# Layer 1 of a two-layer token network by seven half-size products in place of eight, with x1 kept in DRAM

## The chip, the cores and the metric

One core of a Trainium2 chip runs the kernel. The metric is the device time of one execution in microseconds (us). The engines are PE (TensorE), DVE (VectorE), ACT (ScalarE), POOL (GpSimd) and SP (SyncE, which here only issues DMAs).

## The reference

2048 tokens (8 rows of 256) of 1024 features pass two residual layers. Everything is fp32.

```python
# layer 0, per row of 256 tokens, with a language id per row
base = x @ W.T                                  # W 1024 x 1024
logits = x @ Wr.T + 5.0 * one_hot(language_id)  # 8 experts
gates = top-2 of logits, softmax over the two, scattered to 8
h = x @ A.T                                     # A: 8 experts x 16 x 1024
lora = (h * gates) @ B.T
x1 = x + base + 2.0 * lora
# layer 1: one 1024 x 1024 matrix of 16 per row, by adapter id
out = x1 + x1 @ weight[adapter_id].T
```

## The kernel before, in words

**Precision.** PE multiplies in a reduced fp32 (fp32r). Every operand is split into a high part (ACT, a copy that rounds, L487) and a low part (DVE, the difference, L356), and a product is three: high x high, high x low, low x high (`products`, L562 to L566).

**Order of the work.** The tokens go in 4 chunks of 512 (`NCH`). Per chunk PE does the features (L568: h and logits, 4 tiles of 128 tokens x 8 slices, one product with the high part of the tokens against both halves of the factors, 272 columns, and one with the low part, 136 columns), then 8 output tiles of W0 (`base_tile`, L583, 8 x 3 products of 512 columns each) with a low-rank part (`lora_tile`, L600, 3 products each), then layer 2 for two rows: 8 outputs of 8 x 3 products with 512 columns (L621 to L635). x1 comes transposed out of layer 1's PSUM, is split from there by ACT (L507) and DVE (L443), and stays on chip for layer 2. The residuals need no addition: POOL adds the identity to every block of W0 and W1 (`add_ones`, L291).

**Operands.** SP loads a block of 128 rows of a matrix or of the tokens as four DMAs of 128 KB (L244 to L256), into one of four raw slots (`RAW`). DVE turns it in 32 x 32 squares (L349), then the block is split. W0 is loaded and turned again for each chunk; its tiles and those of W1 share a ring of three groups of four blocks. `FIRST`, `AFTER_GATES`, `AFTER_L0` and `after_l1` (L68 to L79) give one order of blocks, which SP, POOL, DVE and ACT all follow; each engine runs its list in order and waits on semaphores.

**Gates.** Once per chunk ACT and DVE turn the feature sums of 4 token tiles into gated h (`make_gates`, L398 to L436); PE transposes it (L611), ACT and DVE split it (L529, L449).

**Start.** 37 identity products in plain fp32 (L561), whose result nobody reads, run until the first operands are there.

## Time and profile before

| | us |
|---|---|
| median of 3 runs | 424.11 (423.76 to 424.12) |
| profiled execution, span from first to last instruction | 423.0 |
| PE busy | 414.4 |
| DVE busy | 314.1 |
| ACT busy | 163.1 |
| POOL busy | 59.5 |

DMA moved 68.52 MB, mean 162 GB/s. No time of the profiled execution other than its span is given. Products overlap: a product's row shows its latency, and the next one starts before it ends, so the rhythm is read from the starts. A busy share near 100% says that an engine always had something in flight, not that it could do no more. A line such as L356 is that of the helper, and stands for all blocks.

### The profile page before, as it was taken

What the parts mean: (1) busy time and instruction counts of PE and PEld (TensorE: products, weight loads), DVE (VectorE), ACT (ScalarE), POOL (GpSimd) and SP (SyncE); (2) the same over time, 40 slices, a digit from 0 to 9 for tenths busy, and PEclk for the clock granted to TensorE, in tenths of its full rate; (3) what the DMA queues carried; (4) which work ended last, traced back from release to release, by engine and by line L of the source; (5) the groups of instructions that cost most, each with busy time, mean ns of one, the idle gap of its engine ahead of it and who ended that gap; (6) DMA issues with size and microseconds to landing.
All of it is one profiled execution on the core that took longest, in us unless ns stands there. A gap on an engine that the chain in (4) does not pass through costs nothing.

```text
span 423.0 us, 6707 instructions
## 1 busy us (share of the span) xinstructions
PE 414.4 (98%) x1978; PEld 349.1 (83%) x1978; DVE 314.1 (74%) x378; ACT 163.1 (39%) x192; POOL 59.5 (14%) x104
## 2 busy tenths in 40 slices
PE   8898999999999999999999999999999999999996
PEld 8786888888898888888888888888889888888885
DVE  3999999999307999998615799999830799994410
ACT  3432544555212455454321445455421245533321
POOL 1021211201200121012110022111310012221000
PEclk9999999999999999999999999999999999999999
DMA  7994677797913666699650576679960356654111
GB/s 173 232 219 120 167 190 200 212 259 203 225 47 99 150 187 180 161 260 249 173 132 0 153 181 188 170 218 252 243 160 26 99 151 175 189 161 123 51 50 50
DMA packets 82542, 68.52 MB, mean 162 GB/s; under 512 B 7986, under 2 KB 82258, under 8 KB 82514
## 3 DMA queue, kind: packets, MB, share of 16 engines
q1 hardware_dynamic: 65618, 59.84, 55.3%
q10 hardware_dynamic: 16896, 8.39, 7.3%
q8 instruction: 8, 0.13, 0.1%
q14 instruction: 20, 0.16, 0.1%
HBM read 59.81 MB, written 8.39 MB: 161 GB/s over the span
## 4 chain that ended last, share of the span: by engine, by line
PE 89%; DVE 3%; DMA 2%; SPq 2%; issue 2%; ACT 0%; POOL 0%; DVEq 0%; ACTq 0%; POOLq 0%
PE banks L564 28%; PE banks L565 28%; PE banks L566 28%; PE banks L577 4%; SPq L255 2%; PE banks L579 1%; DMA raw<-in_L_cond_W_dram 1%; DMA raw<-in_x_dram 1%; DVE turned L349 1%; DVE turned L345 0%; DVE w_lo L356 0%; POOL raw L301 0%; PE gT_ps L611 0%; ACT w_hi L487 0%; DVE gT_lo L449 0%
## 5 line engine op out<-in xcount | busy, mean ns | idle before, releaser
L356 DVE TENSOR_TENSOR w_lo<-turned,w_hi 128x1024 fp32r<-128x1024 f32 x96 | 118.8, 1259 | 38.8 <-ACT w_hi L487 38.0
L487 ACT ACTIVATE w_hi<-turned 128x1024 fp32r<-128x1024 f32 x96 | 101.5, 1062 | 113.1 <-DVE turned L349 103.3
L349 DVE STREAM_TRANSPOSE turned<-raw 128x1024 f32<-128x1024 f32 x113 | 135.3, 1225 | 10.1 <-DMA raw<-in_x_dram 5.1
L301 POOL TENSOR_TENSOR raw<-raw,ident 128x128 f32<-128x128 f32 x96 | 58.4, 608 | 325.9 <-DMA raw<-in_L_cond_weight_dram 182.7
L564 PE MATMUL banks<-xT_hi,w_hi 128*128 128x512 f32 x256 | 100.2, 391 | 0.0
L565 PE MATMUL banks<-xT_lo,w_hi 128*128 128x512 f32 x256 | 99.7, 389 | 0.0
L566 PE MATMUL banks<-xT_hi,w_lo 128*128 128x512 f32 x256 | 99.6, 389 | 0.0
L564 PE MATMUL banks<-w_hi,x1T_hi 128*128 128x512 f32 x256 | 99.6, 389 | 0.0
L565 PE MATMUL banks<-w_lo,x1T_hi 128*128 128x512 f32 x256 | 99.6, 389 | 0.0
L566 PE MATMUL banks<-w_hi,x1T_lo 128*128 128x512 f32 x256 | 99.6, 389 | 0.0
L566 PEld LDWEIGHTS banks<-xT_hi,w_lo 128*128 128x128 f32 x256 | 48.1, 188 | 10.0
L564 PEld LDWEIGHTS banks<-w_hi,x1T_hi 128*128 128x128 f32 x256 | 48.1, 188 | 10.0
L565 PEld LDWEIGHTS banks<-w_lo,x1T_hi 128*128 128x128 f32 x256 | 48.1, 188 | 10.0
L566 PEld LDWEIGHTS banks<-w_hi,x1T_lo 128*128 128x128 f32 x256 | 48.1, 188 | 9.9
L565 PEld LDWEIGHTS banks<-xT_lo,w_hi 128*128 128x128 f32 x256 | 48.1, 188 | 9.7
L564 PEld LDWEIGHTS banks<-xT_hi,w_hi 128*128 128x128 f32 x256 | 48.1, 188 | 9.7
L517 ACT ACTIVATE out_stage<-banks 128x512 f32<-128x512 f32 x32 | 19.1, 597 | 71.3 <-PE banks L566 71.3
L577 PE MATMUL banks<-fac,xT_hi 128*128 128x272 f32 x128 | 30.7, 335 | 2.0 <-DVE fac L389 1.9
L579 PE MATMUL banks<-fac,xT_lo 128*128 128x136 f32 x128 | 29.0, 226 | 0.0
L577 PEld LDWEIGHTS banks<-fac,xT_hi 128*128 128x128 f32 x128 | 24.1, 188 | 2.5 <-DVE xT_lo L356 2.4
L443 DVE TENSOR_TENSOR x1T_lo<-banks,x1T_hi 128x512 fp32r<-128x512 f32 x32 | 21.2, 682 | 5.4 <-ACT x1T_hi L507 5.4
L398 DVE TENSOR_TENSOR h<-banks,h 128x544 f32<-128x544 f32 x4 | 2.9, 719 | 29.5 <-ACT h L499 29.5
(54 smaller groups left out, 197.8 us busy)
## 6 DMA issues: line engine op xcount, KB each, us to landing
raw<-in_L_cond_weight_dram SPq DMA_DIRECT2D x256, 128.0 KB, 2.7
raw<-in_L_cond_W_dram SPq DMA_DIRECT2D x128, 128.0 KB, 3.5
raw<-in_x_dram SPq DMA_DIRECT2D x64, 128.0 KB, 3.3
out_dram<-out_stage ACTq DMA_DIRECT2D x32, 256.0 KB, 3.1
raw<-in_L_cond_A_dram SPq DMA_DIRECT2D x4, 128.0 KB, 3.1
raw<-in_L_cond_B_dram SPq DMA_DIRECT2D x4, 128.0 KB, 4.5
gated<-in_L_cond_Wr_dram SPq DMA_DIRECT2D x4, 8.0 KB
lang_i<-in_itok_B_dram SPq DMA_DIRECT2D x1, 4.0 KB, 2.9
```

Source lines behind the costliest of these rows:

```text
L255: sp.dma_start(raw[c * S:(c + 1) * S, s, :].rearrange("p (q j) -> p q j", q=Q), src[:, :, c * DQ:(c + 1) * DQ]).then_inc(raw_loaded[s], 16)
L301: nc.gpsimd.tensor_tensor(spot, spot, ident[:].rearrange("p (q j) -> p q j", q=Q), ALU.add)\
L349: nc.vector.transpose(turned[:, slot(item, ch, last, 2)].rearrange("p m (q s) -> p q m s", q=Q), raw[:, s, :].rearrange("p (q m j) -> p q ...
L356: nc.vector.tensor_tensor(dest(False, item), turned[:, slot(item, ch, last, 2)], dest(True, item).bitcast(F32), ALU.subtract)\
L443: nc.vector.tensor_tensor(x1T_lo[:, k, :], banks[:, l0_bank(k), :], x1T_hi[:, k, :].bitcast(F32), ALU.subtract).then_inc(x1_done, 1)
L487: nc.scalar.activation(dest(True, item), turned[:, slot(item, ch, last, 2)], ACT.Copy)\
L517: nc.scalar.activation(out_stage[:, s, :].rearrange("p (q k s) -> p q k s", q=Q, k=KH), banks[:, l1_bank(n), :].rearrange("p (k q s) -> p ...
L564: nc.tensor.matmul(ps, st_hi, mv_hi, start=start, stop=False)
L565: nc.tensor.matmul(ps, st_hi, mv_lo, start=False, stop=False)
L566: return nc.tensor.matmul(ps, st_lo, mv_hi, start=False, stop=stop)
L577: nc.tensor.matmul(banks[:, j, 0:2 * FC], xT_hi[:, m, t], fac[:, m, :, :].rearrange("p s f -> p (s f)"), start=m == 0, stop=False)
L579: mm = nc.tensor.matmul(banks[:, j, 0:FC], xT_lo[:, m, t], fac[:, m, 0, :], start=False, stop=m == M - 1)
```

## The change

Layer 1 takes the tokens in 2 spans of 1024. Tokens and W0 are each cut in 2 x 2 quarters of 512 x 512, and the four quarters of the result come from seven quarter products of sums and differences in place of eight, after Strassen and Winograd. A product is 4 slices (k) x 4 tiles (r) of the three fp32r products with 512 columns. Product by product (order 1, 2, 6, 7, 5, 4, 3) they accumulate in 4 main banks and 4 side banks; ACT copies a bank to SBUF where a partial sum is needed twice (`copy_p1`, `copy_u2`, `copy_u3`), DVE adds a side bank to it (`add_p1`, `add_up`). The sums of token quarters (t1 to t4) and of W0 quarters (s1 to s4) are made on POOL (t1, t3, s1, s2, s3) and on DVE (t2, t4, s4), in pieces of 128 x 512. The operands of W0 are made once and stay on chip, high and low; those of the tokens come through a ring of 8 units of 128 x 512. The features run on unsplit fp32 tokens and factors: one fp32 product of 136 columns per slice. The gates of 8 token tiles are made at once. Layer 1's results are split into a stage of two slots (ACT `x1_high`, DVE `x1_low`) and stored by SP in a DRAM tensor, high and low, 512 KB for each of 32 entries; in layer 2, which now runs for all 8 rows after layer 1, ACT's queue loads them, two DMAs of 1 MB per row. Layer 2's own products stay the same in number and shape. The raw slots are 3 in layer 1 and 5 in layer 2. The identity products at the start are 44, and 12 more stand behind the first features.

The core of the diff (additions only; the functions that they replace are those printed above):

```diff
+    WARM = 44
+    FILL = 12
...
+    ORDER = (1, 2, 6, 7, 5, 4, 3)
...
+    RAW = 3
+    RAW1 = 5
+    EARLY = 6
+    LOADS = ([("a",)] + [x_item(0, 0, t) for t in range(XT)] + [("w", m) for m in range(HM)] +
+             [x_item(0, 1, t) for t in range(XT)] + [("w", m) for m in range(HM, M)] + [("b",)] +
+             [x_item(1, h, t) for h in range(2) for t in range(XT)])
...
+    x1_kept = nc.dram_tensor("x1_kept", [M, P, 2, NB * T], F32, kind="Internal").ap()
...
+        stage = sb("stage", [P, 2, D])
...
+            def keep(s, quarter, r):
+                e = quarter_at(s, quarter, r)
+                m = r + (HM if quarter[0] == "2" else 0)
+                t0 = s * 2 * HALF + (HALF if quarter[1] == "2" else 0)
+                sp.wait_ge(x1_lo_done, e + 1)
+                sp.dma_start(x1_kept[m, :, :, t0:t0 + HALF], stage[:, e % 2].rearrange("p (h f) -> p h f", h=2))\
+                    .then_inc(kept[e % 2], 16)
...
+            for item in LOADS[:LOADS.index(x_item(1, 0, RAW))]:
+                load(item)
             sp.wait_ge(adapters_loaded, 16)
+            ids = [sp.value_load(adapters[0:1, r:r + 1], min_val=0, max_val=NA - 1) for r in range(NB)]
+            keep_all(0, "11")
+            keep_all(0, "22")
+            load(x_item(1, 0, 3))
+            load(x_item(1, 1, 0))
+            load(x_item(1, 1, 1))
+            load(x_item(1, 1, 2))
+            keep_all(0, "21")
+            load(x_item(1, 1, 3))
+            keep_all(0, "12")
+            for n in range(RAW):
+                load_w1(n)
...
+            def make_t1(s, t):
+                pool.wait_ge(transposed, TURN_AT[x_item(s, 1, t)] + 1)
+                pool.wait_ge(featured, featured_at(s, 0, t) + 1)
+                pool.wait_ge(lo_done, PIECE_AT[("x", 1, 1, HM - 1) if s else ("xt", t)] + 1)
+                nc.gpsimd.tensor_tensor(half_x(0, t, 0), half_x(1, t, 0), half_x(0, t, 0), ALU.subtract)\
...
+            def make_s3(r):
+                pool.wait_ge(transposed, TURN_AT["w", HM + r] + 1)
+                pool.wait_ge(lo_done, PIECE_AT["wt", r] + 1)
+                a11, a21 = quarter_w(7, r), quarter_w(5, r)
+                nc.gpsimd.tensor_tensor(a11, a11, a21, ALU.subtract).then_inc(s3_done, 1)
+            def make_s2(r):
+                pool.wait_ge(s3_done, r + 1)
+                nc.gpsimd.tensor_tensor(s2_sum(r), quarter_w(4, r), quarter_w(7, r), ALU.subtract).then_inc(s2_done, 1)
...
+            for m in range(HM):
+                add_ones(("w", m))
+            for t in range(XT):
+                make_t1(0, t)
+            for r in range(HM):
+                add_ones(("w", HM + r))
+                make_s3(r)
+                make_s2(r)
+            for t in range(XT):
+                make_t3(0, t)
+            for r in range(HM):
+                make_s1(r)
...
+            turn(x_item(0, 1, 0))
+            low(("wt", 3))
+            turn(x_item(0, 1, 1))
+            make_t2(0, 0)
+            make_t4(0, 0)
+            turn(x_item(0, 1, 2))
+            make_t2(0, 1)
+            make_t4(0, 1)
+            low(("x", 0, 6, 0))
+            turn(x_item(0, 1, 3))
+            make_t2(0, 2)
+            make_t4(0, 2)
+            low(("x", 0, 6, 1))
+            turn(("w", 4))
+            make_t2(0, 3)
+            make_t4(0, 3)
+            low(("x", 0, 6, 2))
+            turn(("w", 5))
+            low(("x", 0, 6, 3))
+            make_s4(0)
+            turn(("w", 6))
+            low(("u", 6, 0))
+            make_s4(1)
+            add_p1(0, 0)
+            turn(("w", 7))
+            low(("u", 6, 1))
+            make_s4(2)
+            add_p1(0, 1)
+            low(("u", 6, 2))
+            make_s4(3)
+            low(("u", 6, 3))
+            add_p1(0, 2)
+            add_p1(0, 3)
+            lows("u", 7)
+            low(("x", 0, 7, 0))
+            low(("x", 0, 7, 1))
             dve.wait_ge(setup, 4)
...
+            def x1_high(s, quarter, r):
+                e = quarter_at(s, quarter, r)
+                if quarter == "21":
+                    act.wait_ge(lora_done, e + 1)
+                    src = main_bank(s, r)
+                else:
+                    act.wait_ge(summed_up, added_at(s, quarter, r) + 1)
+                    src = (sums2 if quarter == "12" else sums13)[:, r]
+                if e >= 2:
+                    act.wait_ge(kept[e % 2], e // 2 * 16)
+                nc.scalar.activation(stage[:, e % 2, 0:HALF].bitcast(F32R), src, ACT.Copy).then_inc(x1_hi_done, 1)
...
+            def load_x1(row):
+                if row == 0:
+                    act.wait_ge(steps, product_end(1, 4))
+                elif row == 1:
+                    act.wait_ge(steps, product_end(1, 3))
+                else:
+                    act.wait_ge(l1_ready, (row - 1) * 2 * TT)
+                for slot in range(2):
+                    act.wait_ge(kept[slot], (8 if row < NB // 2 else 16) * 16)
+                for low in range(2):
+                    act.dma_start(x1_part(row, low).bitcast(F32),
+                                  x1_kept[:, :, low, row * T:(row + 1) * T].rearrange("m p t -> p m t"))\
+                        .then_inc(x1_loaded[row % 2], 16)
...
+            def step(s, i, k, r, bank, first):
+                ps = bank.rearrange("p (t f) -> p t f", t=XT)
+                u_hi, u_lo = (u_part(i, r, low)[:, k * P:(k + 1) * P] for low in range(2))
+                x_hi, x_lo = x_part(s, i, k, 0), x_part(s, i, k, 1)
+                nc.tensor.matmul(ps, u_hi, x_hi, start=first and k == 0, stop=False, skip_group_check=True)
+                nc.tensor.matmul(ps, u_hi, x_lo, start=False, stop=False, skip_group_check=True)
+                nc.tensor.matmul(ps, u_lo, x_hi, start=False, stop=k == HM - 1, skip_group_check=True)\
+                    .then_inc(steps, 1)
...
+            def turn_gated(s):
+                pe.wait_ge(gate_steps, (s + 1) * GATE_STEPS)
+                pe.wait_ge(p1_added, HM * s + 2)
+                for j in range(GT):
+                    turn_g = nc.tensor.transpose(gT_ps(s)[:, j // XT, (j % XT) * P:(j % XT + 1) * P],
+                                                 h_all[:, j, 0:ER], ident[:])
                 turn_g.then_inc(gT_turned, 1)
+            def whole_piece(s, i, k):
+                pe.wait_ge(lo_done, PIECE_AT["x", s, i, HM - 1 if (s, i) == (0, 6) else k] + 1)
+                if s == 0 and k == 0:
+                    pe.wait_ge(lo_done, PIECE_AT["u", i, HM - 1] + 1)
+            def first_products():
+                for r in range(HM):
+                    pe.wait_ge(lo_done, PIECE_AT["wt", r] + 1)
+                    for k in range(HM):
+                        step(0, 1, k, r, main_bank(0, r), True)
+                features(0, 1)
+                for r in range(HM):
+                    pe.wait_ge(h_copied, 1 + r // 2)
+                    for k in range(HM):
+                        step(0, 2, k, r, side_bank(0, r), True)
+            def product(s, i, wait_bank, first, bank, ks=range(HM)):
+                for k in ks:
+                    whole_piece(s, i, k)
+                    for r in range(HM):
+                        if k == 0:
+                            wait_bank(r)
+                        step(s, i, k, r, bank(s, r), first)
+            def span(s):
+                product(s, 6, lambda r: pe.wait_ge(p1_copied, HM * s + r + 1), False, main_bank)
+                turn_gated(s)
+                product(s, 7, lambda r: pe.wait_ge(u2_copied, HM * s + r + 1), False, main_bank, range(HM - 1))
+                pe.wait_ge(gT_done, s + 1)
+                pe.wait_ge(lo_done, PIECE_AT["b",] + 1)
+                for r in range(HM):
+                    pe.wait_ge(p1_added, HM * s + r + 1)
+                    lora(s, "11", r)
+                product(s, 7, None, False, main_bank, range(HM - 1, HM))
+                product(s, 5, lambda r: pe.wait_ge(summed_up, added_at(s, "11", r) + 1), True, side_bank)
+                for r in range(HM):
+                    lora(s, "22", r)
+                product(s, 4, lambda r: pe.wait_ge(u3_copied, HM * s + r + 1), False, main_bank)
+                for r in range(HM):
+                    lora(s, "21", r)
+                product(s, 3, lambda r: pe.wait_ge(summed_up, added_at(s, "22", r) + 1), False, side_bank)
+                pe.wait_ge(lo_done, PIECE_AT["bd",] + 1)
+                for r in range(HM):
+                    lora(s, "12", r)
+            features(0, 0)
+            for _ in range(FILL):
+                nc.tensor.matmul(banks[:, 0, 0:P], ident[:], ident[:], start=True, stop=True)
+            first_products()
+            span(0)
+            features(1, 0)
+            features(1, 1)
+            product(1, 1, lambda r: pe.wait_ge(summed_up, added_at(0, "12", r) + 1), True, main_bank)
+            product(1, 2, lambda r: pe.wait_ge(h_copied, 3 + r // 2), True, side_bank)
+            span(1)
+            for row in range(NB):
+                pe.wait_ge(x1_loaded[row % 2], (row // 2 + 1) * 2 * 16)
+                for j in range(2):
+                    g = 2 * row + j
+                    pe.wait_ge(w1_ready, (g + 1) * HM)
                     for t in range(TT):
+                        o = g * TT + t
+                        if o < HM:
+                            pe.wait_ge(x1_lo_done, quarter_at(1, "21", o) + 1)
+                        elif o < 2 * HM:
+                            pe.wait_ge(summed_up, added_at(1, "12", o - HM) + 1)
+                        else:
+                            pe.wait_ge(l1_copied, o - 7)
+                        tok = slice(t * P, (t + 1) * P)
                         for m in range(M):
+                            x_hi, x_lo = x1_part(row, 0)[:, m, tok], x1_part(row, 1)[:, m, tok]
+                            w_hi, w_lo = w1_part(g, 0)[:, m, :], w1_part(g, 1)[:, m, :]
+                            nc.tensor.matmul(l1_bank(o), x_hi, w_hi, start=m == 0, stop=False)
+                            nc.tensor.matmul(l1_bank(o), x_hi, w_lo, start=False, stop=False)
+                            mm = nc.tensor.matmul(l1_bank(o), x_lo, w_hi, start=False, stop=m == M - 1)
                         mm.then_inc(l1_ready, 1)
```

DVE's order behind the gates, for each span: pieces of product 5; four `add_up` of quarter 11; `x1_low` of 11 mixed with pieces of product 4; four `add_up` of 22; `x1_low` of 22 mixed with pieces of product 3; `x1_low` of 21; in span 0 four turns of the next tokens, in span 1 the first six blocks of W1 in between; and after product 3 `add_up` and `x1_low` of quarter 12. ACT's order mirrors it. From block 9 of W1 on DVE turns block n and subtracts block n-1.

## Rows read from the trace of the kernel before

**Rows 1.** The page, part 1: busy time, share of the span and instructions of each engine.

```profile
PE 414.4 (98%) x1978; PEld 349.1 (83%) x1978; DVE 314.1 (74%) x378; ACT 163.1 (39%) x192; POOL 59.5 (14%) x104
```

**Rows 2.** Everything PE waited for in the whole span: us in total, times, longest.

```profile
PE banks L577 <- DVE fac L389: 1.9, 1, 1.9
...
PE banks L564 <- DVE gT_lo L449: 0.7, 1, 0.7
...
PE gT_ps L611 <- DVE gated L436: 0.5, 1, 0.5
```

**Rows 3.** Timeline of PE inside a product, and the end of the span: start us, us, what.

```profile
126.21 0.39 PE L566 MATMUL banks<-xT_hi,w_lo 128*128 128x512 f32 x1
...
128.93 0.39 PE L566 MATMUL banks<-xT_hi,w_lo 128*128 128x512 f32 x1
...
419.31 0.60 ACT L517 ACTIVATE out_stage<-banks 128x512 f32<-128x512 f32 x1 [4.84 <-PE banks L566]
```

**Rows 4.** Timeline of PE in the feature products of one chunk: first and last of 30 steps.

```profile
117.67 0.33 PE L577 MATMUL banks<-fac,xT_hi 128*128 128x272 f32 x1
...
124.77 0.33 PE L577 MATMUL banks<-fac,xT_hi 128*128 128x272 f32 x1
```

**Rows 5.** Identity products before the work: two stretches; all of them, ns min/median/max.

```profile
1.68 3.15 PE L561 MATMUL gT_ps<-ident 128*128 128x128 f32 x13 [1.68 <-POOL ident L287]
...
7.74 4.52 PE L561 MATMUL gT_ps<-ident 128*128 128x128 f32 x39
...
L561 PE MATMUL gT_ps<-ident x74: 275/275/582, 1.7 to 12.7; 128*128 128x128 f32 x74
```

**Rows 6.** Groups of instructions: line engine op, names, shapes, count; busy us, mean ns; idle before.

```profile
L349 DVE STREAM_TRANSPOSE turned<-raw 128x1024 f32<-128x1024 f32 x113 | 135.3, 1225 | 10.1 <-DMA raw<-in_x_dram 5.1 <-DMA raw<-in_L_cond_A_dram 1.4 <-POOL raw L301 1.2
...
L356 DVE TENSOR_TENSOR w_lo<-turned,w_hi 128x1024 fp32r<-128x1024 f32 x96 | 118.8, 1259 | 38.8 <-ACT w_hi L487 38.0
...
L487 ACT ACTIVATE w_hi<-turned 128x1024 fp32r<-128x1024 f32 x96 | 101.5, 1062 | 113.1 <-DVE turned L349 103.3 <-ACT out_stage L517 7.8
...
L443 DVE TENSOR_TENSOR x1T_lo<-banks,x1T_hi 128x512 fp32r<-128x512 f32 x32 | 21.2, 682 | 5.4 <-ACT x1T_hi L507 5.4
```

**Rows 7.** Timeline of the start and of the first gates: start us, us, what.

```profile
3.04 1.85 SPq L255 DMA_DIRECT2D raw<-in_L_cond_A_dram  x4
...
5.10 1.25 DVE L349 STREAM_TRANSPOSE turned<-raw 128x1024 f32<-128x1024 f32 x1 [5.10 <-DMA raw<-in_x_dram]
...
8.12 1.25 DVE L349 STREAM_TRANSPOSE turned<-raw 128x1024 f32<-128x1024 f32 x1 [1.40 <-DMA raw<-in_L_cond_A_dram]
...
30.21 0.49 DVE L400 TENSOR_TENSOR logits<-h,bias 128x32 f32<-128x32 f32 x1
...
33.64 0.69 DVE L436 TENSOR_TENSOR gated<-h,gates 128x512 f32<-128x512 f32 x1
```

**Rows 8.** POOL additions begun beside a DVE subtraction, and all 96 of them (min/median/max ns).

```profile
20.81 1.22 DVE L356 TENSOR_TENSOR w_lo<-turned,w_hi 128x1024 fp32r<-128x1024 f32 x1
...
21.21 1.14 POOL L301 TENSOR_TENSOR raw<-raw,ident 128x128 f32<-128x128 f32 x1 [2.81 <-DMA raw<-in_L_cond_W_dram]
...
43.34 1.23 DVE L356 TENSOR_TENSOR w_lo<-turned,w_hi 128x1024 fp32r<-128x1024 f32 x1
...
43.91 0.97 POOL L301 TENSOR_TENSOR raw<-raw,ident 128x128 f32<-128x128 f32 x1 [1.84 <-DMA raw<-in_L_cond_weight_dram]
...
L301 POOL TENSOR_TENSOR raw<-raw,ident x96: 454/464/1471, 17.8 to 385.5; 128x128 f32<-128x128 f32 x96
```

**Rows 9.** DMA queues (packets, MB, share of 16 engines) and two stretches of 20 us.

```profile
q1 hardware_dynamic: 65618, 59.84, 55.3%
...
q10 hardware_dynamic: 16896, 8.39, 7.3%
...
80.00:100.00 20.00, 20.00 (x90) 16.57 (x89) 19.53 (x17) 11.01 (x13) 2.63 (x5) 1.00 1.01 260
...
390.00:410.00 20.00, 20.00 (x90) 16.58 (x89) 6.24 (x6) 5.58 (x7) 0.00 (x0) 1.00 0.14 40
```

1199 lines of the change are left out of this document (778 added, 421 removed).

## The prediction

> **What bounds the kernel now.** I read the busy shares first, then what PE waited for, then PE's own rhythm, and last the engines that feed it. PE is busy 98% of the span and DVE 74% [rows 1]; busy time alone says little, but PE's waits sum to under 5 us, of which only two small ones lie behind the first real product at 14.8 us [rows 2]. So the kernel is a line of matrix products without gaps, and its time is their number times their rhythm. The rhythm: twelve products of 512 columns lie between the starts 126.21 and 128.93, 0.2267 us each (the 0.39 of a row is latency, the next one starts before it ends) [rows 3]. A pair of feature products (272 and 136 columns) takes 7.10/30 = 0.2367 us [rows 4].
>
> The span of 423.0 is then: 14.8 before the first feature, 128 pairs x 0.2367 = 30.3, 1632 products x 0.2267 = 370.0 (4 chunks x (8 tiles x 8 x 3 for layer 1, 8 x 3 low-rank, 8 outputs x 8 x 3 for layer 2)), 3.9 from the last product (about 419.1) to the end [rows 3], and 4.0 left for 16 transposes, two waits of 1.2 [rows 2] and joints.
>
> **What the change removes.** Layer 1 is 2 spans x 7 products x 16 steps x 3 = 672 products in place of 768; low-rank 2 x 4 x 4 x 3 = 96 and layer 2's 768 stay. 96 x 0.2267 = **21.8 us** less on the bounding engine. The granted clock was 1.00, the 2.4 GHz level, in the stretches read [rows 9], so I price all of them at this rhythm.
>
> **Features.** 128 products of 136 columns on plain fp32, in place of 128 pairs. The identity products are the fp32 ones the trace has: each is two records, and 39 records take 4.52 us less the last one's 0.275, 0.112 each, 0.223 for 128 columns [rows 5]. By columns that is 0.237 for 136, so 30.4 us: no change. The ends are 0.223 (28.5 us) and double the rhythm, 60 us, which nothing in rows 5 once settled suggests.
>
> **Start.** 44 identity products in place of 37. The first 29 records start before 7.74 (of before's 74, ended at 12.9, 45 fit at 0.112 from 7.74 on) [rows 5], the other 59 take 6.6: PE is free at 14.3, and the A factors and first tokens (landed by 8.1, turned by 9.4 [rows 7]) are ready, without a hi/lo split now. FILL adds 12 x 0.223 = 2.7. Sum without any new wait: 14.3 + 30.4 + 2.7 + 1536 x 0.2267 = 348.2 + transposes 1.8 + joints 1.0 + tail 3.9 = **402.3**.
>
> **What DVE and POOL add before product 6.** Features, fill, products 1 and 2 keep PE until 54.0. By then DVE must have done 17 turns x 1.225 = 20.8, 8 subtractions of 1024 x 1.26 = 10.1, 20 of 512 and 2 bank sums x 0.68 = 15.0 [rows 6], 1.1 of small work, after starting at 5.1 and waiting some 2.6 for loads (6.3 to 8.1 is one such gap [rows 7]): 54.7. That is 0.7 late at best. But 12 additions on POOL (t1, s3, s2) lie in the chain. Their price: 0.46 for 128 columns [rows 8]; 512 columns cost between 0.46 and 4 x 0.46 = 1.84. I take 1.4 (0.15 fixed, 0.31 per 128, from the 0.31 by which a blocked addition outlasts its blocker). And they exclude DVE's two-input work: an addition begun at 21.21 ended at 22.35, 0.32 after DVE's subtraction (to 22.03); one of 43.91 ended at 44.88, 0.31 after 44.57 [rows 8]. If all twelve hold DVE up, less the 6 turns (7.4) that may lie beside them: 54.7 + 16.8 - 7.4 = 64.1; at 1.84 each, 69.4. The order alternates turn and subtraction, so most collide: I take 61.5, a wait of **7.5** (0.7 to 15.4).
>
> The Trainium skill (SBUF — State Buffer, Who interferes with whom) says that a DVE instruction with two SBUF inputs and a GpSimd one that reads SBUF exclude each other for the whole instruction, whoever came first. It speaks against this change: without it the wait would be near 0.7 to 3. The trace shows DVE holding POOL off; that POOL holds DVE off for 1.4 it can't show, its additions being short.
>
> **Gates.** During product 6 (48 x 0.2267 = 10.9) DVE does two bank sums, six pieces of 512 (5.4 together), loses about 2 to POOL's t3, and makes the gates of eight tiles at once. Four took 30.21 to 34.33 [rows 7]; eight cost two more rounds of max and index and double the last multiply, 5.9. 13.3 against 10.9: **2.4** of wait (0 to 5).
>
> **The later products.** Each gives PE 13.6 us with its low-rank part; DVE has 16 pieces x 0.68 = 10.9 and in two of them 5 more of turns; ACT about 16 x 0.6. Product 4 waits for copies that stand on ACT behind a store of x1 through a two-slot stage (some 4 us each turn). It fits by about 1 us; at nothing, and 6 if the cover goes (1 us at each of six joints). SP issues the 32 stores of x1 in the same queue as its loads, each behind a wait for DVE's subtraction; the loads behind them are needed a product or more later, so I price them at nothing (if that cover goes, a load's 1.85 + 3 us). In span 1 DVE has 32 pieces and 11 blocks of W1: 34.5 of 40.8.
>
> **Layer 2.** PE takes 8 blocks x 12 x 0.2267 = 21.8 per row, DVE 8 x (1.225 + 1.26) = 19.9 [rows 6], so a lead grows slowly. At its start DVE has blocks 5 to 7 and eight sums of x1 before it while PE needs block 7 after 10.9 us: **2** (0 to 5).
>
> DMA: before 68.5 MB; now W0 once (-12.6) and x1 written and read (+33.6), 89. In layer 2 a row takes 4.19 MB of W1, 2.10 of x1 and 1.05 of output, 7.34 MB in 21.8 us, 337 GB/s. The loads moved 59.84 MB in 55.3% of the span, 256 GB/s at full share; the outputs 8.39 MB in 7.3%, 272 GB/s; 20 us at share 1.01 brought 260, while outputs alone did 40 at 0.14, 286 per full share [rows 9]. But the saturated loads are 32-partition pieces issued at 128 KB per 0.46 us [rows 7], 283 GB/s, so their rate may be SP's; x1 comes in whole tiles from ACT's queue. Five raw slots (13.6 us of PE) and what lead the finished groups have cushion a shortage. I take **3** (0 to 30).
>
> The Trainium skill (DMA: Bandwidth & Descriptors, Where 436 GB/s comes from) puts loads from HBM at about 358 GB/s per core; a row would then take an estimated 20.5 us and DMA bound nothing. No stretch of 20 us here shows it.
>
> **Sum.** 402.3 + 7.5 + 2.4 + 2 + 3 = 417.2 of span. The runs' median is 424.11 where the profiled span is 423.0; the 1.1 carries over: **418**.
>
> **Rivals.**
> A, the early chain is hidden: POOL's 512-column additions cost under 1 us or DVE slips between them. For: DVE alone would be 0.7 late. Against: rows 8. 402.3 + 0.7 + 0 + 2 + 1 + 1.1 = 407. Chance 0.13.
> B, layer 2 becomes bound by DMA; slower than before. It decides where the mixed traffic stays under about 305 GB/s: 28.3 MB of W1, 14.7 of x1 and 7.3 of output in some 165 us. At 256 and 272 GB/s these take 168 + 27 = 195 us, 30 more: 418 - 3 + 30 = 445; halfway, 430. For: the highest 20 us are 260. Against: SP's issue rate explains that ceiling too. Chance 0.27, likeliest 432.
> C, the hand-overs of products do not fit: 6 us at the joints and 3 more at layer 2's start, 427. For: margins of 1 us through ACT, DVE and a store. Against: neither engine is over 86% there. Chance 0.10.
> The forecast itself, 411 to 424: 0.50. That fewer products run is fixed by the code and no rival.
>
> **Chances.** 0.2% is what a measurement can tell, 423.3 to 425.0. Faster: 0.13, most of the forecast (0.46) and a little of C: 0.61. Same: 0.06. Slower: most of B and C, 0.33. Range 407 to 436: it leaves out A's lower half and B's upper third. The forecast's own range is 411 to 424.
>
> **What would show it.** PE products 1632 down to 1536 with starts still 0.227 apart; feature starts 0.237; PE's longest wait before product 6 on a DVE subtraction, product 6 starting near 61; POOL's 512-column rows near 1.4 alone and longer beside DVE; a wait of some 2 us before the gate transposes; in layer 2 hardly a gap. I am wrong if PE waits in layer 2 for x1 or W1 with DMA share near 1.0 (B), if product 6 starts by 55 (A), if waits of 1 us repeat at each product (C), or if the granted clock falls after the early wait, which would stretch the rhythm.

## The result and the profile after

After: **460.08 us** (median of 4 runs, 458.41 to 462.78); before, on the same chip, 424.12 (423.76 to 424.46). The ratio is 1.0852, 95% interval 1.0815 to 1.0888: 36 us slower where 6 faster were forecast. The profiled execution has a span of 458.3 us. The ratios go by fast executions alone; the medians of long_runs and all_three below hold one slow execution each, and without it they are 457.92 and 457.30.

The page of the kernel after: busy time by engine (beside [rows 1]), the granted clock in 40 slices of 11.5 us, the DMA queues (beside [rows 9]), the chain by engine.

```profile
PE 408.2 (89%) x1920; PEld 341.1 (74%) x1920; DVE 317.6 (69%) x400; ACT 167.6 (37%) x239; POOL 92.0 (20%) x108
...
PEclk9999958999999999999999769986999998899999
...
q1 hardware_dynamic: 60288, 63.99, 50.7%
q10 hardware_dynamic: 33746, 25.21, 20.2%
...
PE 31%; DMA 25%; DVE 17%; SPq 10%; issue 7%; POOL 4%; ACT 2%; ACTq 2%; DVEq 0%; POOLq 0%
```

PE's share falls from 98% to 89%, and the chain that was PE's before is now split over DMA, DVE, SP's queue and PE. The clock row dips in four places (slices 6 and 7, 23 and 24, 27 and 28, 34 and 35). What PE waited for (beside [rows 2]; us in total, times, longest):

```profile
PE banks L1213 <- DMA tokens<-x_kept: 14.3, 4, 8.4
PE banks L1116 <- DVE weights L528: 13.6, 2, 13.4
PE banks L1213 <- DVE weights L647: 11.1, 1, 11.1
PE banks L1136 <- DVE stage L603: 2.4, 1, 2.4
```

These are four places: product 6 (13.4), the gates (2.4), the second column group of layer 2's first row (11.1, called the start gap below: the first group runs from 244.3 without a wait) and the rest of layer 2 (14.3, which with short waits beside them make 16.0 between the starts of products). PE's timeline around product 6, and one gap of layer 2 (start us, us, what; beside [rows 3]):

```profile
53.32 0.39 PE L1118 MATMUL banks<-weights 128*128 128x512 f32 x1
67.12 0.77 PE L1116 MATMUL banks<-ring,weights 128*128 128x512 f32 x1 [13.41 <-DVE weights L528]
...
68.11 0.63 PE L1118 MATMUL banks<-ring,weights 128*128 128x512 f32 x1
68.54 0.63 PE L1116 MATMUL banks<-ring,weights 128*128 128x512 f32 x1
...
71.38 0.40 PE L1117 MATMUL banks<-ring,weights 128*128 128x512 f32 x1
71.61 0.39 PE L1118 MATMUL banks<-ring,weights 128*128 128x512 f32 x1
...
311.71 0.79 PE L1213 MATMUL banks<-weights,tokens 128*128 128x512 f32 x1 [8.42 <-DMA tokens<-x_kept]
```

After an idle stretch the products start 0.427 us apart (68.11 to 68.54), nearly twice the 0.2267 of [rows 3], and from 71.4 on 0.227 again. The windows show the clock (window, us, busy us of PE, PEld, DVE, ACT, POOL with counts, granted clock, DMA share, GB/s):

```profile
60.00:70.00 10.00, 2.88 (x7) 2.33 (x8) 9.90 (x10) 2.71 (x5) 9.92 (x7) 0.50 0.19 55
...
266.00:272.00 6.00, 5.60 (x13) 4.49 (x14) 5.64 (x7) 3.68 (x5) 1.44 (x1) 0.50 0.82 242
286.00:302.00 16.00, 16.00 (x72) 13.24 (x71) 12.77 (x12) 7.12 (x9) 2.30 (x5) 1.00 1.13 266
312.00:316.00 4.00, 4.00 (x10) 3.13 (x10) 3.65 (x4) 1.54 (x2) 1.03 (x2) 0.50 1.14 360
386.00:391.50 5.50, 5.24 (x12) 4.13 (x13) 3.62 (x4) 1.12 (x3) 1.92 (x3) 0.50 1.12 331
...
300.00:420.00 120.00, 105.66 (x440) 85.66 (x439) 93.16 (x80) 50.75 (x60) 25.45 (x39) 0.93 1.12 303
```

A clock of 0.50 is the 1.2 GHz level; PE had stood idle 13.6, 11.2, 8.6 and 3.3 us before it in these four windows. Some 48 products run at it, 0.20 more each: about 10 us. The length of the wait alone does not tell whether this happens: in no_round_trip_tiny below PE waits 2.8 and 3.4 us and the granted clock stays 1.00, in long_runs a wait of 2.0 us is followed by 9 products at half rate. The last row is the state of layer 2: DMA share above 1 without a break, 303 GB/s. That share is no measure of the rate: it is 1.13 at 266 GB/s too, between 286 and 302, where PE does not wait.

The trace tells which transfer is late there. For row 4, W1's last block of the first column group is ready at 352.6; the low part of x1's row, issued at 338.8 when its tile has come free, lands at 361.0, and PE starts at 361.1. So W1 is some 8 us early, and a load of x1 takes 22 us, as long as PE takes for a row.

**The balance.** 402.3 of PE work as forecast + 13.6 + 2.6 + 2.5 (three small gaps at 147, 150 and 165) + 11.2 + 16.0 + 10 of half-rate products = 458.2, against 458.3. (The kernels below that hardly wait come out 1.4 to 2 under such a sum, so the 402.3 is high by that much, and some small waits fill it here.)

### The profile page after: what moved, and what is told of

Same layout as the page of the kernel before. It is cut to its first block, busy times and chain, and to the rows that moved or that the text cites. A ratio compares the mean times of both kernels' runs of the same rounds, so it can differ in the third digit from the quotient of the medians.

```text
span 458.3 us, 5994 instructions
## 1 busy us (share of the span) xinstructions
PE 408.2 (89%) x1920; PEld 341.1 (74%) x1920; DVE 317.6 (69%) x400; ACT 167.6 (37%) x239; POOL 92.0 (20%) x108
## 3 DMA queue, kind: packets, MB, share of 16 engines
q1 hardware_dynamic: 60288, 63.99, 50.7%
q10 hardware_dynamic: 33746, 25.21, 20.2%
## 4 chain that ended last, share of the span: by engine, by line
PE 31%; DMA 25%; DVE 17%; SPq 10%; issue 7%; POOL 4%; ACT 2%; ACTq 2%; DVEq 0%; POOLq 0%
SPq L359 10%; DMA raw<-in_L_cond_weight_dram 9%; DMA x_kept<-stage 6%; PE banks L1213 5%; PE banks L1215 5%; PE banks L1214 5%; DMA tokens<-x_kept 5%; PE banks L1116 5%; PE banks L1117 5%; PE banks L1118 5%; DMA ring_f<-in_L_cond_weight_dram 3%; DVE stage L631 2%; DVE weights_f L641 2%; DVE tokens_f L514 2%; DMA raw<-in_x_dram 2%
## 5 line engine op out<-in xcount | busy, mean ns | idle before, releaser
L1213 PE MATMUL banks<-weights,tokens 128*128 128x512 f32 x176 | 72.5, 412 | 23.7 <-DMA tokens<-x_kept 12.6
L1116 PE MATMUL banks<-ring,weights 128*128 128x512 f32 x192 | 76.0, 396 | 14.6 <-DVE weights L528 13.4
L641 DVE STREAM_TRANSPOSE weights_f<-raw 128x1024 f32<-128x1024 f32 x42 | 52.0, 1240 | 36.3 <-POOL raw L444 36.1
L1214 PE MATMUL banks<-weights,tokens 128*128 128x512 f32 x176 | 71.6, 407 | 0.0
L1215 PE MATMUL banks<-weights,tokens 128*128 128x512 f32 x176 | 71.3, 405 | 0.0
L958 ACT ACTIVATE weights<-weights_f 128x1024 fp32r<-128x1024 f32 x44 | 45.7, 1057 | 58.7 <-DVE weights_f L641 29.3
L647 DVE TENSOR_TENSOR weights<-weights_f,weights 128x1024 fp32r<-128x1024 f32 x44 | 52.7, 1198 | 13.9 <-ACT weights L958 13.7
L1213 PEld LDWEIGHTS banks<-weights,tokens 128*128 128x128 f32 x176 | 35.1, 199 | 32.8 <-DMA tokens<-x_kept 13.9
L1116 PEld LDWEIGHTS banks<-ring,weights 128*128 128x128 f32 x192 | 36.6, 190 | 23.0 <-DVE weights L528 13.8
L1118 PE MATMUL banks<-ring,turned_w 128*128 128x512 f32 x128 | 49.8, 389 | 0.0
L1117 PE MATMUL banks<-tokens,weights 128*128 128x512 f32 x128 | 49.8, 389 | 0.0
L1215 PEld LDWEIGHTS banks<-weights,tokens 128*128 128x128 f32 x176 | 34.9, 199 | 7.7
L1214 PEld LDWEIGHTS banks<-weights,tokens 128*128 128x128 f32 x176 | 35.1, 199 | 7.4
L1213 PE MATMUL banks<-turned_w,tokens 128*128 128x512 f32 x80 | 31.3, 392 | 2.6 <-DMA tokens<-x_kept 1.8
L1109 PE MATMUL banks<-fac,tokens_f 128*128 128x136 f32 x256 | 30.9, 280 | 1.2 <-DVE tokens_f L514 1.0
L1215 PE MATMUL banks<-turned_w,tokens 128*128 128x512 f32 x80 | 31.1, 389 | 0.0
L1214 PE MATMUL banks<-turned_w,tokens 128*128 128x512 f32 x80 | 31.1, 389 | 0.0
## 6 DMA issues: line engine op xcount, KB each, us to landing
tokens<-x_kept ACTq DMA_DIRECT2D x16, 1024.0 KB, 15.3
```

The source lines that it names most:

```text
L641: nc.vector.transpose(w1_turn(n).rearrange("p (m q s) -> p q m s", m=M, q=Q), raw_tile(SLOT[item]).rearrange("p (q m j) -> p q m j", q=Q, ...
L647: nc.vector.tensor_tensor(w1_dest(n, 1), w1_turn(n).rearrange("p (m f) -> p m f", m=M), w1_dest(n, 0).bitcast(F32), ALU.subtract).then_inc ...
L958: nc.scalar.activation(w1_dest(n, 0), w1_turn(n).rearrange("p (m f) -> p m f", m=M), ACT.Copy)\
L1109: mm = nc.tensor.matmul(ps, xT[:, m, :], fac[:, m, 0:FC], start=m == 0, stop=m == M - 1)
L1116: nc.tensor.matmul(ps, u_hi, x_hi, start=first and k == 0, stop=False, skip_group_check=True)
L1117: nc.tensor.matmul(ps, u_hi, x_lo, start=False, stop=False, skip_group_check=True)
```

## The experiments

Every kernel starts from the one after and is measured beside the one before (424.1 to 424.6). Those that leave work out are named as such.

**Twelve of sixteen loads left out (x1_two_rows).** Rows 2 to 7 of x1 are not loaded; layer 2 multiplies what is in the tiles.

```
 def load_x1(row):
+    if row >= 2:
+        return
```

> Leaves out the loads of x1 for rows 2 to 7 (layer 2 multiplies rows 0 and 1 again and again); 12.6 MB less in layer 2, nothing else changes. Theory D (the 16 DMA engines are full in layer 2): PE's gaps from 280 us on, 16.0 us together, and the half-rate products behind them go, the wait at layer 2's start shrinks a little; DMA share well under 1.12; time 436 to 442. Rival L (W1 is late because its loads wait for only five slots and each takes long, whatever the traffic, or because DVE and ACT can't keep up): 455 or more, the gaps stay.

Measured: 440.79, ratio 1.0363 (1.0321 to 1.0406), 19.3 less. (PE's wait for these loads goes with them.) Its window:

```profile
300.00:380.00 80.00, 80.00 (x355) 66.26 (x354) 73.02 (x64) 41.02 (x47) 18.12 (x34) 1.00 1.06 272
```

PE is busy without a gap from the second row on. 12.6 MB at 303 GB/s would be 41 us; the gain is 19.3, the 16.0 of gaps and their slow products, and no more, since PE bounds from there. The share is not "well under 1.12" as expected: 1.13 from 300 to 340 and 1.06 over the window, falling to 0.88 and 0.85 only from 360 on. The start gap stays (11.8).

**Whole partitions (whole_partitions).** Each block is loaded by four DMAs of 128 partitions, one column quarter each, in place of four of 32 partitions.

```
-for c in range(Q):
-    sp.dma_start(raw_tile(s)[c*S:(c+1)*S, :] ..., rows[:, :, c*DQ:(c+1)*DQ])
+for q in range(Q):
+    sp.dma_start(raw_tile(s)[:, q*DQ:(q+1)*DQ], rows[:, q, :].rearrange("s (c j) -> c s j", c=Q))
```

> Every block of x, W0, W1 and A is loaded as four DMAs over all 128 partitions (a fourth of the columns each) in place of four over 32 partitions; bytes, packets and issues stay. Rival S (it is the 32-partition shape that holds the loads to some 300 GB/s): rate in layer 2 above 330 GB/s, time 440 to 450. Theory D (the engines are full by packets, whatever the shape): 456 to 461.

Measured: 715.68, ratio 1.6881 (1.6818 to 1.6943), which no expectation came near. The same bytes on SP's queue, at half the share, and a chain that is SP's:

```profile
q1 hardware_dynamic: 56016, 63.97, 25.3%
...
SPq 60%; PE 12%; DMA 9%; DVE 8%; issue 7%; POOL 2%; ACT 1%; POOLq 0%; DVEq 0%; ACTq 0%
```

Four issues took 6.1 us in place of 1.85 [rows 7]. So this kernel is bound by issuing, with DMA's engines busy less than half the time, and says nothing of a ceiling by bytes: the form can't replace the old one, and the question went to other runs.

**POOL's additions made tiny (tiny_pool_sums).** The twelve additions t1, s3 and s2 cover one column, not 512; all waits stay (two are added so that t3 and s1 still follow them).

```
-nc.gpsimd.tensor_tensor(a11, a11, a21, ALU.subtract)
+nc.gpsimd.tensor_tensor(a11[:, 0:1], a11[:, 0:1], a21[:, 0:1], ALU.subtract)
```

> The additions t1, s3 and s2 on POOL work on one column in place of 512 (the sums are left out), so POOL hardly holds DVE up. Theory: product 6 starts near 55 in place of 67.1, no half-rate products behind it; the gates' wait of 2.6 stays; time 14 to 16 less, 443 to 446. Rival V (DVE's own work sets it): product 6 still starts at 60 or later, time 452 or more. Rival Q (layer 2 starts earlier and only waits longer for DMA): product 6 at 55, but 455.

Measured: 447.17, ratio 1.0561 (1.051 to 1.0611), 12.9 less, a little over the 443 to 446 expected. Product 6 starts at 56.4 in place of 67.1, and 8 products behind it still run at half rate, which was not expected. So these twelve additions cost 10.7 of the 13.6 us. The other 3 are not DVE's own work either, for POOL's next four additions (t3, in full here) now begin at 51.1:

```profile
51.11 6.33 POOL L458 TENSOR_TENSOR tokens_f<-tokens_f 128x512 f32<-128x512 f32 x4
```

Three of DVE's last subtractions beside them take 1.33, 1.76 and 1.56 where 0.65 to 0.68 is usual, 2.7 us more. Without that product 6 would start near 53.7, an estimate from these rows, and PE is free for it at 53.2.

**Both (two_rows_tiny).** 

> Both edits together: x1 of rows 2 to 7 not loaded, and the POOL sums on one column. If the two losses are separate they add: 458 - 20 - 15 = 423 to 427. If both only shift the wait at layer 2's start (11.2 us), more than 432.

Measured: 427.72, ratio 1.0076 (1.0054 to 1.0099). 32.4 less than after, about the sum of the two gains (19.3 + 12.9 = 32.2): with DMA relieved, what is won before product 6 reaches the end in full.

```profile
PE banks L1218 <- DVE weights L650: 12.8, 1, 12.8
```

The largest wait left is the start gap.

**Loads before stores (loads_before_stores).** SP issues W1's blocks 6 to 8 before the stores of quarter 21; ACT issues x1's row 0 after that quarter. Full work.

```
 load_w1(5)
-keep_all(1, "21")
-for n in range(EARLY, EARLY + RAW):
-    load_w1(n)
+load_w1(6); load_w1(7); load_w1(8)
+keep_all(1, "21")
 load_w1(9)
```

> SP issues W1's blocks 6, 7 and 8 before the stores of quarter 21 of span 1 (after: behind them, at 243.4), and ACT issues the load of x1's row 0 behind that quarter's last two copies, so that it no longer shares the engines with the stores that the two stage slots wait for. Nothing is left out. Theory O (order): PE's wait at layer 2's start, 11.2 us, falls under 4. Whether the time falls with it tells what bounds layer 2: if DMA was idle or badly used before, 446 to 451; if the engines' total is the bound, the gaps inside layer 2 grow by what the start gives and the time stays at 456 or more.

Measured: 457.32, ratio 1.0762 (1.0727 to 1.0797). The wait only changed hands:

```profile
PE banks L1215 <- DMA tokens<-x_kept: 26.0, 5, 13.8
```

The load of block 8 waits for a turn at 234.8, the stores are now stuck behind it, the two-slot stage fills, and row 0 of x1 is issued at 243.9.

**Long runs (long_runs).** x1 lies in DRAM as row, partition, part, so that a load has runs of 8 KB, not 1 KB. 

> x1 lies in DRAM as row, partition, part, slice, token: a load of a row reads 8 KB at a stretch in place of 1 KB (each store becomes two DMAs of 1 KB runs in place of one of 2 KB runs). Bytes stay. Theory P (what DMA costs in layer 2 goes by packets): the rate in layer 2 rises over 320 GB/s and its gaps shrink by 8 to 12, time 446 to 452. Theory B (by bytes, the rate stays at 303): 456 to 461.

Measured: 458.45, ratio 1.0741 (1.0685 to 1.0798). The stretch of layer 2:

```profile
300.00:420.00 120.00, 109.92 (x464) 88.47 (x463) 88.26 (x77) 49.14 (x57) 25.76 (x38) 0.97 1.10 297
```

33,746 packets on ACT's queue became 19,410, a load of x1 lands in 10.7 in place of 15.3 (medians), and the total is 297 GB/s where it was 303. Longer runs of x1 don't lift the total. Now that x1 lands sooner W1 comes late in its place: the last block of row 5 is ready at 395.58 and PE takes it up at 395.64, after 1 us idle, where in the kernel after W1 was 8 to 10 us early.

**The additions on DVE (sums_on_dve).** t1 of span 0, s3 and s2 run in full on DVE. 

> t1 of span 0, s3 and s2 move from POOL to DVE, in full, so that no POOL addition stands in DVE's way before product 6; nothing is left out. DVE has 12 x 0.68 = 8.2 us more of its own. Theory K (the two engines exclude each other): DVE loses its doubled subtractions (8 rows of 1.7 where 0.68 is the work, 8 us) and the handovers, so product 6 starts at 62 to 65 in place of 67.1, time 2 to 5 less. Rival (DVE's work bounds): product 6 at 70 or later, time 461 or more.

Measured: 457.01, ratio 1.08 (1.0747 to 1.0853).

```profile
PE banks L1134 <- DVE weights L517: 15.3, 2, 14.8
```

Product 6 starts at 68.1, a miss. But the edit did not clear POOL out of the way as it was meant to. POOL's t3 and s1, which ran from 63.1 on in the kernel after, move forward with nothing before them and stand beside DVE again:

```profile
47.12 6.39 POOL L457 TENSOR_TENSOR tokens_f<-tokens_f 128x512 f32<-128x512 f32 x4
...
50.58 1.78 DVE L517 TENSOR_TENSOR ring<-ring_f,ring 128x512 fp32r<-128x512 f32 x1
```

Six of DVE's subtractions before product 6 take 1.66 to 1.78, 6.3 us over their undisturbed time, beside the 8.2 of the twelve new ones. So this run does not tell whether DVE's work alone would fill the time; a version with t3 and s1 held back was not run. The time is 3.1 under the kernel after, inside the 2 to 5 expected, but the two intervals overlap. The gates' wait is gone.

**The last three together (all_three).** 

> The three edits together. If they are separate: 458 less the sum of what each gave, around 438. If DMA's total bounds layer 2, what the first and third give earlier is lost again in layer 2 and only the long runs count: 447 or more. Below 424 only if the long runs remove all gaps of layer 2.

Measured: 457.99, ratio 1.0771 (1.0749 to 1.0792), no better than loads_before_stores or sums_on_dve alone (457.32, 457.01); 300 to 420 runs at share 1.10 and 294 GB/s.

**No round trip (no_round_trip).** All stores and loads of x1 are left out; layer 2 multiplies what its tiles hold. ACT takes a stage slot as soon as DVE has subtracted from it.

```
-sp.wait_ge(x1_lo_done, e + 1)
-sp.dma_start(x1_kept[m, :, :, t0:t0 + HALF], ...).then_inc(kept[e % 2], 16)
+return
...
 def load_x1(row):
+    return
```

> Left out: every store of x1 to DRAM and every load of it; layer 2 multiplies what its tokens tiles hold. All other work, the full additions on POOL among it, stays. Theory T (the total of the transfers sets layer 2, and the stores in SP's queue set layer 2's start): the gaps at layer 2's start (11.2) and in layer 2 (16.0) go with their half-rate products, what stays is 402.3 of PE work, 13.6 + 1.9 before product 6, 2.6 at the gates, 3 of joints and 1.1 = 424 to 428. Rival O (layer 2's start waits for DVE and ACT's own order of work, not for the late W1 blocks behind the stores): a gap of 5 to 11 stays at the start, 431 to 436.

Measured: **420.46**, ratio 0.9902 (0.9885 to 0.9918), below the 424 to 428 expected (the three small gaps at products' joints go too). All that PE waits for:

```profile
PE banks L1114 <- DVE weights L526: 13.8, 1, 13.8
PE banks L1134 <- DVE stage L601: 2.9, 1, 2.9
PE banks L1095 <- POOL ident L434: 1.7, 1, 1.7
```

Nothing is left in layer 2. The round trip costs 460.1 - 420.5 = 39.6 us.

**The same with tiny additions (no_round_trip_tiny).** 

> The same with the additions t1, s3 and s2 on one column in place of 512. Theory T: product 6 starts near 56.4 as with the short additions alone, so 11 to 12 us less than without the round trip: 411 to 416, which beats the kernel before and shows the 96 products that were saved. Rival O: 5 to 11 more at layer 2's start.

Measured: **408.93**, ratio 0.9634 (0.9616 to 0.9652), a little under the 411 to 416 expected. 15.6 less than before: the 21.8 of the 96 products, less 2.8 before product 6 and 3.4 at the gates. The saving is real and the rhythm is as forecast.

**The same bytes from two queues (half_x1_rows, half_w1_blocks).** 6.3 MB less, once by leaving out the low parts of x1's rows 2 to 7, once by leaving out half the row groups of 24 blocks of W1.

```
-for low in range(2):
+for low in range(2 if row < 2 else 1):
```
```
+qs = 2 if item[0] == "w1" and item[1] >= 16 and item[1] % 2 else Q
 ...
-    sp.dma_start(raw_tile(s)..., rows[:, :, c*DQ:(c+1)*DQ])
+    sp.dma_start(raw_tile(s)...[:, 0:qs], rows[:, 0:qs, c*DQ:(c+1)*DQ])
```

> Of rows 2 to 7 of x1 only the high part is loaded: 6.3 MB less on ACT's queue, all else as in the kernel after. Theory T: at about 303 GB/s 6.3 MB are 20.8 us, more than the 16.0 of gaps in layer 2, so these nearly vanish: 441 to 446, about the same as without all loads of these rows (440.8). Rival Q (the loads of x1 are late by their own latency, issued only when a row is done, whatever the bytes): at most the half of 19.3 us, 450 or more.

> The same 6.3 MB taken from another queue: of the 24 odd blocks of W1 from number 16 on only half the pieces are loaded (two of four row groups, runs of 1 KB as before), x1 is loaded in full. Theory T (a byte is a byte, whichever queue brings it): the same time as with half of x1, 441 to 446, within 3 us of it. Rival Q: x1's latency stays, 455 or more.

Measured: 442.30 (ratio 1.0437, 1.0408 to 1.0466) and 444.91 (1.0461, 1.0423 to 1.0499), 2.6 apart. Half of x1, then half of W1:

```profile
300.00:380.00 80.00, 79.26 (x347) 64.64 (x347) 68.48 (x59) 38.07 (x44) 20.86 (x31) 1.00 1.13 291
```
```profile
300.00:380.00 80.00, 76.96 (x333) 63.18 (x332) 69.23 (x61) 39.36 (x45) 25.65 (x32) 0.98 1.07 298
```

The time comes out nearly alike whosever bytes go. In the second kernel x1's loads come in time from row 3 on (one wait of 3.0 before row 2), although they have all their bytes and are issued as soon after the row before as in the kernel after; the low part of row 4 lands in 16 us, not 22. That rules out a latency of their own and leaves what moves beside them. With long_runs, where the sooner x1 only made W1 late, it is the total that bounds.

A byte is not a byte for the engines, though: the share is 1.13 in the first and 1.07 in the second. And the total that DMA holds depends on what moves. Without any load of x1 (no_x1_loads, below) W1 and the outputs run at the same share at 273 GB/s (267 to 289 in windows of 20 us, x1_two_rows included):

```profile
300.00:380.00 80.00, 80.00 (x355) 66.24 (x354) 74.54 (x65) 40.94 (x47) 17.73 (x35) 1.00 1.13 273
```

So 303 is the rate of this mix, and no figure for other ones. A third tokens tile, with which x1 could be issued a row earlier, was not tried.

**What makes the start gap (no_x1_loads).** All stores stay, all loads of x1 are left out. 

> All stores of x1 stay, in SP's queue as in the kernel after; left out is every load of it (rows 0 to 7), so layer 2 multiplies what its tokens tiles hold. Theory S (layer 2 starts late because W1's blocks 6 to 9 are issued behind the stores): the gap at layer 2's start stays at about 11, nothing in layer 2 after it, 420.5 of the kernel without the round trip + 11 + 1 of half rate = 430 to 435. Rival L (it is the load of x1's rows 0 and 1 that keeps W1's blocks from landing): the gap falls below 4 and the time to 421 to 425.

Measured: 429.93, ratio 1.0142 (1.0127 to 1.0157). The time lies at the edge of the band for the stores, but the gap does not: it is two gaps now, 5.2 in all.

```profile
PE banks L1213 <- DVE turned_w L647: 3.2, 1, 3.2
...
PE banks L1213 <- DVE weights L647: 1.7, 1, 1.7
```

Neither theory holds alone. Row 1 of layer 2 starts 27.1 us after row 0 here (243.2 to 270.3), 37.0 after it in the kernel after (244.3 to 281.3), and 21.8 without the round trip (242.2 to 264.0): of 15.2 us lost in the first row, 9.9 go with the loads of x1 (some 2.8 of them as half-rate products, which this kernel does not have there) and 5.3 with its stores. The trace shows what the loads did. W1's block 6, issued and then taken up by POOL:

```profile
239.69 6.35 SPq L359 DMA_DIRECT2D raw<-in_L_cond_weight_dram  x12
...
244.94 0.46 POOL L444 TENSOR_TENSOR raw<-raw,ident 128x128 f32<-128x128 f32 x1 [13.69 <-DMA raw<-in_L_cond_weight_dram]
```

5.3 us from issue to use, and issued at 239.7; in the kernel after 12.0 us, and issued at 243.4, 1.7 us behind the load of x1's row 1.

**The stores on ACT (stores_on_act).** Full work; ACT issues each store one item after its copy, and SP's queue holds only loads.

```
+def put_kept(left=0):
+    while len(pending) > left:
+        ...
+        act.wait_ge(x1_lo_done, e + 1)
+        act.dma_start(x1_kept[m, :, :, t0:t0 + HALF], ...).then_inc(kept[e % 2], 16)
 def high(p):
     ...
+    put_kept()
```

> Full work; the 32 stores of x1 are issued by ACT, one item of its order later, and no longer stand between SP's loads. Theory S: layer 2's start gap falls from 11.2 to 2 to 5. But theory T (total bytes at some 300 GB/s from 235 us on) gives most of it back in layer 2: 450 to 457. If S alone held and DMA had room: 449 or less. If ACT's waits for DVE's subtractions cost at the products' joints: gaps of 1 us at each of them, over 460.

Measured: 450.55, ratio 1.0623 (1.0607 to 1.0638), the best full version, 9.5 under the kernel after. Waits, and the stretch of layer 2:

```profile
PE banks L1229 <- DMA tokens<-x_kept: 15.9, 5, 4.5
...
PE banks L1229 <- issue: 6.2, 1, 6.2
```
```profile
300.00:420.00 120.00, 109.60 (x461) 89.45 (x462) 94.30 (x80) 50.71 (x59) 25.70 (x40) 0.96 1.12 307
```

The three small gaps at products' joints are gone, and layer 1 is through at 240.3 in place of 244.3: 4.0 of the 8.3 us of span. The first row hardly gains: its wait is now in two pieces, 4.7 before it (x1's row 0) and 6.3 before row 1, which starts 34.7 after the end of layer 1 in place of 37.0. The expected "2 to 5" holds for the first piece alone. The second piece (the wait of 6.2 that the profile puts down to nothing) is not for x1, whose row 1 was issued at 238.4 and had landed by 260.1. W1's block 11 had landed by 255.0, but DVE ends its subtraction only at 274.89, and PE starts at 274.99. DVE takes its items in order, and stood before one of x1's:

```profile
261.82 0.64 ACT L946 ACTIVATE stage<-sums 128x512 fp32r<-128x512 f32 x1 [9.22 <-DMA x_kept<-stage]
...
262.49 0.69 DVE L626 TENSOR_TENSOR stage<-sums,stage 128x512 fp32r<-128x512 f32 x1 [7.32 <-ACT stage L946]
```

So the stores still cost here, by another way: a copy waits for a stage slot until an earlier store has landed, which takes long while the queues are full (303 GB/s from 230 to 245 and 296 from 245 to 265). A stage of more than two slots was not tried.

**The same with DMA relieved (stores_on_act_less_dma).** Without rows 2 to 7 of x1 and with the tiny additions. 

> The same, with the loads of x1's rows 2 to 7 left out and the additions t1, s3 and s2 on one column: the kernel of 427.7 with its stores on ACT. DMA has room in layer 2 here, so theory S is alone: the start gap of 13.0 falls to 2 to 5, 416 to 420. Rival L: the gap stays over 10, 426 or more.

Measured: 424.20, ratio 0.9999 (0.9983 to 1.0014), between the two bands and 3.5 under the 427.72 of two_rows_tiny. The start gap of 13.0 became a wait of 5.2 for x1's row 0 and another of 5.4 before row 1, which again ends with DVE's subtraction of W1's block 11 (264.85; PE at 264.95) and not with a load:

```profile
PE banks L1234 <- issue: 5.4, 1, 5.4
PE banks L1234 <- DMA tokens<-x_kept: 5.2, 1, 5.2
```

So the stores' place in SP's queue is a small part of it. The larger is how long all transfers take to land in this stretch: W1's block in the kernel after, x1's row 0 and the stores of the stage here. Whether x1's row 0 could be loaded in the idle time of layer 1 was not tried.

## Why the prediction was wrong

**Right.** The products (1920 records in all, the 96 gone), their rhythm of 0.2267 at full clock, and the first features. no_round_trip_tiny gives the base: 402.3 + 6.2 of waits = 408.5 of span, measured 407.1. The gates: 2.4 forecast, 2.6 measured. Features:

```profile
L1109 PE MATMUL banks<-fac,tokens_f 128*128 128x136 f32 x256 | 30.9, 280 | 1.2 <-DVE tokens_f L514 1.0
```

256 records for 128 products, and 30.9 busy where 30.4 were forecast from the two-record rule of [rows 5].

**Step 1, product 6: 7.5 forecast, 13.6 measured, and 1.9 of slow products behind it.** The mechanism was right, the size of the collision was not. One group of POOL's additions, rows of the timeline around product 6, and four additions of span 1 with no such subtraction of DVE beside them (start us, us, what):

```profile
L463 POOL TENSOR_TENSOR turned_w_f<-turned_w_f 128x512 f32<-128x512 f32 x4 | 6.5, 1634 | 5.9 <-DVE turned_w_f L514 5.9
```
```profile
35.78 1.63 POOL L451 TENSOR_TENSOR tokens_f<-tokens_f 128x512 f32<-128x512 f32 x1 [1.78 <-DVE tokens_f L514]
...
36.30 1.65 DVE L551 TENSOR_TENSOR tokens_f<-tokens_f,ring_f 128x512 f32<-128x512 f32 x1
...
53.45 1.25 DVE L514 STREAM_TRANSPOSE turned_w_f<-raw 128x1024 f32<-128x1024 f32 x1 [1.60 <-POOL raw L444]
...
157.63 5.04 POOL L456 TENSOR_TENSOR tokens_f<-tokens_f 128x512 f32<-128x512 f32 x4
```

Undisturbed an addition takes 1.29 (the last row: four, one behind the other), a little less than the 1.4 I took. The twelve show 1.6 to 2.2, because each began beside a subtraction of DVE and was held up itself. DVE's subtraction begun beside one takes 1.65 and ends (37.95) half a us after it (37.41), where an undisturbed one takes 0.69. So the exclusion goes both ways: POOL holds DVE off as DVE held POOL off in [rows 8]. That is what the Trainium skill (SBUF — State Buffer, Who interferes with whom) says, and the half that the trace before could not show is here. Beside the twelve, eight of DVE's subtractions take 1.65 to 1.78 in this way, some 8.3 us more in all, where my sum came to 6.8 more for all twelve additions. I had let the six turns lie free beside the additions; the row of 53.45 shows the turn itself waiting 1.6 for POOL's addition of the identity, which stands in POOL's queue behind the long ones. The turns of W0's second half wait 2.9 in all. And I had counted twelve additions, where three of t3's four also begin before product 6 (the first at 63.1). DVE's own lateness, 0.7 by my sum, comes to some 0.5 by tiny_pool_sums, so nearly all of the 13.6 is the collision. The wait lies inside the range of its term (0.7 to 15.4).

**Step 2, layer 2's transfers: 3 forecast, 16.0 measured.** This is the largest of the steps that failed: the forecast let the transfers hide behind PE, and rival B, given 0.27, is what happened. The mixed traffic holds 303 GB/s, just under the 305 named as the point of decision, and a row's 7.34 MB then take 24.2 us, not 21.8: 2.4 a row for seven rows, 17 us, against 16.0 in gaps. The doubt I had put against B, that the 256 to 272 GB/s of [rows 9] was SP's issuing rate, was half true: 303 is more than 260, but only with x1 in the mix; W1 and the outputs alone are at 267 to 289 at a full share, and no run shows whether it is SP's issuing that holds them there. It was no reason to take 3; the working gave a point of decision at 305 with all measured rates under it, and the forecast should have stood on that side. Even so B's price for layer 2 was 30, not 16, and its likeliest 432 meets this step alone (418 - 3 + 16 = 431); the rest of the way to 460 is in the other steps. The Trainium skill (DMA: Bandwidth & Descriptors, Where 436 GB/s comes from) gives about 358 GB/s per core for loads from HBM. Here, with loads and stores mixed, no stretch of 80 us or more exceeded 309, with x1 in runs of 1 or 8 KB, so the measurement decides.

**Step 3, layer 2's first row: 2 forecast, 11.2 measured.** I had named the place (PE needs block 7 after 10.9 us) and only counted DVE's work before it. SP's timeline, and then POOL's and DVE's at the gap:

```profile
225.87 2.68 SPq L359 DMA_DIRECT2D raw<-in_L_cond_weight_dram  x4
234.22 9.01 SPq L390 DMA_DIRECT2D x_kept<-stage  x4
243.41 7.16 SPq L359 DMA_DIRECT2D raw<-in_L_cond_weight_dram  x12
```
```profile
255.39 0.45 POOL L444 TENSOR_TENSOR raw<-raw,ident 128x128 f32<-128x128 f32 x1 [23.05 <-DMA raw<-in_L_cond_weight_dram]
255.87 1.25 DVE L641 STREAM_TRANSPOSE weights_f<-raw 128x1024 f32<-128x1024 f32 x1 [13.18 <-POOL raw L444]
```

DVE was not too busy, it stood idle for 13 us. Four stores hold SP's queue for 9 us, each behind a wait for DVE and a stage slot (ACT's copy for the third stands 9.1, until the first, issued at 234.2, lands at 240.1; x1's row 0 is loading beside it until 238.8); the next block is issued at 243.4 and lands 12 us later, since 245 to 265 runs at share 1.04 with x1's row 1, issued at 241.8, in it. Both terms had been set to nothing: the stores "at nothing", and the load at a landing of 3 us. By no_x1_loads the loads of x1 weigh more (9.9 of 15.2) than the stores, and by both runs with the stores on ACT moving them to another queue mends little of it.

**Step 4, the clock: about 10 us, not priced.** The prediction named it as what would make it wrong, but gave it no term. The long waits were paid for a second time: 11.2 us of idle, then 14 products at half rate.

**The joints** cost 2.5 in span 1, forecast at nothing; they vanish with the stores on ACT, so they too came from the stores' place in SP's queue.

By size: 16.0 for 3, 11.2 for 2 and 13.6 for 7.5 are 28.3 of the 41.1 us between 417.2 and the span of 458.3; 10 are clock and 2.5 joints. The first two, the joints and most of the clock come from the round trip, which no_round_trip prices at 39.6 together. Without it the change is worth 4 us (424.49 to 420.46), and 15.6 if the additions cost nothing too. None of the full versions comes near the kernel before.

## What to carry over

Saving products buys nothing if the saving is paid in bytes: work out the bytes per stretch of PE time, and if the rate needed is above any that a trace has shown, forecast the transfer bound. Price a store that waits for a computed value by the tightest load behind it in its queue, and each load, and each store whose buffer is needed again, by its landing time in full queues, not in idle ones. When an edit takes work off an engine, look what that engine does next: POOL's later additions moved forward and collided in place of the ones taken away. A wait on PE can cost more than its length: behind four waits of 3.3 to 13.6 us the products ran at half rate.

## What was not expected of the hardware

Loading a block by column quarters with 128 partitions each, the same bytes, raised the issue from 0.46 to 1.5 us and took the share of SP's queue from 50.7% to 25.3% of a span 1.56 times as long, 715.68 us. DMA shares of 1.10 to 1.12 were held for 120 us at 294 to 307 GB/s whatever the run length of x1 or the queue that issued its stores, and a share of 1.13 for 80 us at 273 without x1. A GpSimd addition of 512 columns takes 1.29 us undisturbed, nearly three times one of 128 (0.46). Beside a VectorE subtraction of two SBUF inputs both grow: the addition to 1.6, the subtraction from 0.69 to 1.65 to 1.78.
